# A transformer tower on one core: weight halves, output jobs and base jobs placed anew ahead of and inside the first attention turn

## The reference, cut to what matters

```python
h = s4d_kernel(log_dt, x, B, inv_A_real, A_imag, 1024)     # 64 x 128 x 1024, one row per channel and column of x
a = layernorm(h)                                            # 64 blocks of 128 tokens, 1024 wide
q, k, v = a @ wq.T, a @ wk.T, a @ wv.T                      # 32 query heads, 8 key/value heads, 32 wide
q, k = rope(q), rope(k)
h = h + softmax(causal(q @ k.T / sqrt(32))) @ v @ wo.T      # 128 tokens: every causal key is allowed
y = layernorm(h)
alpha = softmax(log(prior) + y @ router_W.T + router_b)     # 4 active experts
h = h + y @ W_base.T + b_base + sum_e alpha_e * (y @ lora_A_e.T @ lora_B_e.T) * 2
```

## Time and profile before

| | us |
|---|---|
| median of 3 runs | 2940.04 |
| lowest, highest | 2939.99, 2941.34 |
| the profiled execution | 2938.84 |
| its span, first to last instruction | 2937.2 |
| PE busy | 2827.0 (96%) |
| DVE busy | 2436.1 (83%) |
| ACT busy | 1917.3 (65%) |
| POOL busy | 1974.4 (67%) |

### The profile page before, as it was taken

One profiled execution on the slowest core, in us unless ns is written; L12 is line 12 of the kernel. 1 busy time (PEld: TensorE's weight loads), 2 busy tenths in 40 slices (PEclk: granted clock), 3 DMA queues, 4 the chain that ended last, 5 costly groups with the idle time before them and its releaser, 6 DMA issues.

```text
span 2937.2 us, 62768 instructions
## 1 busy us (share of the span) xinstructions
PE 2827.0 (96%) x17444; PEld 1403.3 (48%) x17444; DVE 2436.1 (83%) x8643; ACT 1917.3 (65%) x5982; POOL 1974.4 (67%) x1735
## 2 busy tenths in 40 slices
PE   6788899999999999999999999999999999999987
PEld 5665444444444444444444444444444444444433
DVE  8987788888888888888888888888888888888873
ACT  7987666666666666666666666666666666666662
POOL 4543676777677776777777776677766777677763
PEclk9999899999999999999999999999999999999999
DMA  7884676666666666666666666666666666666652
GB/s 227 241 220 136 136 155 146 149 147 146 151 144 149 147 147 148 148 149 147 148 150 142 148 146 154 148 144 148 145 154 147 146 148 144 151 146 147 144 130 65
DMA packets 1220852, 442.66 MB, mean 151 GB/s; under 512 B 1167120, under 2 KB 1175568, under 8 KB 1220640
## 3 DMA queue, kind: packets, MB, share of 16 engines
q1 hardware_dynamic: 1220640, 440.69, 66.2%
HBM read 88.22 MB, written 67.11 MB: 53 GB/s over the span
## 4 chain that ended last, share of the span: by engine, by line
PE 59%; DVE 15%; issue 9%; POOL 7%; ACT 7%; DMA 1%; SPq 0%; DVEq 0%; ACTq 0%; POOLq 0%
PE bank_b L1763 29%; PE bank_a L1763 16%; PE bank_c L1763 6%; ACT probs L1337 4%; DVE heads L1543 3%; DVE probs L1489 3%; POOL p_hl L1250 3%; PE score L1728 3%; POOL probs L1246 3%; PE pv L1752 2%; PE kps L565 1%; POOL rope_a L1256 1%; DVE share L1498 1%; POOL xy_hl L1265 1%; DMA tok_h<-kout 1%
## 5 line engine op out<-in xcount | busy, mean ns | idle before, releaser
L1337 ACT ACTIVATE probs<-probs,negmax 128x128 f32<-128x128 f32 x2048 | 789.8, 387 | 253.3 <-DVE negmax L1489 253.2
L1250 POOL TENSOR_TENSOR p_hl<-probs,p_hl 128x512 f16<-128x512 f32 x512 | 615.5, 1202 | 340.3 <-ACT p_hl L1346 338.1
L1246 POOL TENSOR_TENSOR probs<-probs,rsum 128x512 f32<-128x512 f32 x512 | 556.6, 1087 | 221.2 <-DVE rsum L1500 220.1
L1763 PE MATMUL bank_a<-qkv_hi,xt 128*128 128x512 f16 x2048 | 652.1, 380 | 1.0 <-DMA xt<-xy_hl 1.0
L1489 DVE CUSTOM_DVE_ANT_0 probs<-score,table,scal 128x128 f32<-128x128 f32 x2048 | 597.5, 347 | 45.4 <-issue 44.8
L1763 PE MATMUL bank_b<-b_hi,yt 128*128 128x512 f16 x2016 | 630.9, 379 | 0.0
L1346 ACT ACTIVATE p_hl<-probs 128x512 f16<-128x512 f32 x512 | 319.8, 625 | 417.6 <-POOL probs L1246 417.6
L1543 DVE TENSOR_TENSOR heads<-rope_a,heads 128x512 f16<-128x512 f32 x320 | 397.8, 1259 | 29.9 <-ACT heads L1367 29.9
L1763 PE MATMUL bank_b<-o_hi,at_hi 128*128 128x512 f16 x1024 | 389.7, 381 | 1.5 <-ACT at_hi L1352 1.5
L1763 PE MATMUL bank_b<-o_lo,at_hi 128*128 128x512 f16 x1024 | 389.9, 381 | 0.0
L1763 PE MATMUL bank_b<-o_hi,at_lo 128*128 128x512 f16 x1024 | 389.7, 381 | 0.0
(11 more groups left out here) (209 smaller groups left out, 4598.8 us busy)
## 6 DMA issues: line engine op xcount, KB each, us to landing
hin<-tok_h SPq DMA_DIRECT2D x64, 512.0 KB, 3.3
r<-tok_h SPq DMA_DIRECT2D x64, 512.0 KB, 3.9
out_dram<-r SPq DMA_DIRECT2D x63, 512.0 KB, 3.0
tok_h<-kout SPq DMA_DIRECT2D x60, 512.0 KB, 6.1
probs_t<-p_hl SPq DMA_TRANSPOSE x512, 3.1
xc<-in_x_dram SPq DMA_DIRECT2D x32, 128.0 KB, 4.5
raw_a<-in_L_attn_wq_dram SPq DMA_DIRECT2D x4, 1024.0 KB, 8.9
raw_b<-in_L_attn_wo_dram SPq DMA_DIRECT2D x8, 512.0 KB, 5.5
```

Of the source, the lines that this page charges most:

```text
L1246: TT(x, x, rsum[:, u % 4].unsqueeze(2).to_broadcast([P, GR, T]), ALU.mult).then_inc(s_norm, 1)
L1250: TT(p_hl[:, u % 2, 1], probs[:, u % 4], p_hl[:, u % 2, 0], ALU.subtract).then_inc(s_plo, 1)
L1337: ins = A(probs[:, u % 4, g], probs[:, u % 4, g], ACT.Exp, bias=negmax[:, u % 4, g:g + 1], scale=-1.0, accum_out=sums[:, u % 4, g:g + 1])
L1763: ins = MM(bank, x(c), w[:, c, cols], start=(c == 0 and i == 0), stop=(c == KC - 1 and i == 2))
```

## The change

Four things are moved; no instruction is added or removed in number, apart from waits.

- DVE makes the low halves of jobs 10 to 13 in `begin`, so ahead of the norm statistics of block 0.
- `pe_close` holds jobs 30 to 35 (`LATE` = 36). The output jobs 36 to 39 move into turn 0, which then has 20 jobs, in the units as 1, 1, 4, 3, 3, 3, 3, 2. PE runs them at the end of a unit, behind its product (`jobs_of`). Jobs 36 to 41 use the banks 2 and 3 in turn, where 38 and 39 had the banks of the scores.
- The statistics of the base weight move from DVE's turn -1 to unit 0 of turn 0, `spread` behind job 37 at the end of unit 1, and `powers(2)` to unit 1.
- In turns 0 and 1 (`spare`) the second query product has 1 step ahead of `scores(3)`, 3 behind it and 4 behind `scores(4)`.

```diff
+    LATE = MID + 6
+    per_slot = (1, 1, 4, 3, 3, 3, 3, 2)
+    SLOTS = [(LATE + sum(per_slot[:k]), LATE + sum(per_slot[:k + 1])) for k in range(8)]
...
         if j < MID:
             return (0, 1, 5, 7)[j % 4]
-        return (j - MID) % 4 if j < J_B else 2 + (j - J_B) % 3
+        if j < LATE:
+            return (j - MID) % 4
+        return 2 + (j - LATE) % 2 if j < J_B else 2 + (j - J_B) % 3
...
             if b == -1 and k == "last":
-                Prep.high(act, MID + 4, J_B)
+                Prep.high(act, MID + 4, LATE)
             if b == 0 and k != "norm" and k != "last":
-                Prep.high(act, J_B + 2 * k, J_B + 2 * k + 2)
+                Prep.high(act, *SLOTS[k])
...
-                low(4, 10)
+                low(4, 14)
 
             def after():
-                low(10, J_O)
+                low(14, J_O)
...
                 if b == -1 and k == "last":
                     low(MID, MID + 4)
+                if b == -1 and k == "end":
+                    low(MID + 4, LATE)
+                if b == 0 and k == 0:
                     dve.wait_ge(s_sums, NO)
                     V.tensor_reduce(mx[:, 2:3], part_max[:, 0:NO], AX_X, ALU.max).then_inc(s_mx, 1)
                     columns(2)
-                if b == -1 and k == "end":
-                    low(MID + 4, J_B)
-                if b == 0 and k == 0:
+                if b == 0 and k == 1:
                     powers(2)
...
                 if b == 0 and isinstance(k, int):
-                    low(J_B + 2 * k, J_B + 2 * k + 2)
+                    low(*SLOTS[k])
...
-            Prep.turn(pe, MID, J_B)
+            Prep.turn(pe, MID, LATE)
...
-                    if u == 0 and not some(b):
-                        prep.spread(pe, 2)
-                    if not some(b):
-                        prep.turn(pe, prep.jb + 2 * u, prep.jb + 2 * u + 2)
+
+                def jobs_of(u):
+
+                    if attention and not some(b):
+                        prep.turn(pe, *prep.slots[u])
+                        if u == 1:
+                            prep.spread(pe, 2)
...
                 if qkv:
                     q(0, 0, 6)
+                jobs_of(1)
...
                 if rest:
                     attend(1)
-                if qkv:
-                    q(1, 0, 5)
+                spare = attention and not finish
+                if qkv:
+                    q(1, 0, 1 if spare else 5)
+                jobs_of(2)
 
                 if attention:
                     scores(3)
                 if qkv:
-                    q(1, 5, 8)
+                    q(1, 1 if spare else 5, 4 if spare else 8)
...
+                jobs_of(3)
 
                 if attention:
                     scores(4)
+                if qkv and spare:
+                    q(1, 4, 8)
...
+                jobs_of(4)
```

More of the change, by code:

```diff
@@ L662, in prepare_weights @@
         done_a, done_c, done_score, done_pv = last_a + 1, last_c + 1, (last[0] + 1, last[1] + 1), last[4] + 1
-        jb, jend, mid = J_B, J_END, MID
+        jb, jend, mid, slots = J_B, J_END, MID, SLOTS
         @staticmethod
@@ L1830, in turn @@
                     kv(0, 7)
+                jobs_of(0)
                 if attention:
@@ L1884, in turn @@
                                         id16[:, :]).then_inc(s_zt, 1)
+                jobs_of(5)
                 if attention:
@@ L1896, in turn @@
                     wo(1, 0, 1)
+                jobs_of(6)
                 if attention:
@@ L1901, in turn @@
                     wo(1, 1, 8)
+                jobs_of(7)
             turns(pe, turn)
```

## The result

| | us |
|---|---|
| before, median of 19 runs (lowest, highest) | 2940.81 (2939.69, 2945.58) |
| changed, median of 19 runs (lowest, highest) | 2947.61 (2945.43, 2950.06) |
| ratio, 95% interval | 1.0023 (1.0017 to 1.0030) |
| changed, profiled execution and its span | 2948.72, 2947.0 |

The changed kernel is 6.8 us slower. That is inside the range of 2938.0 to 2948.0, 3.5 above the forecast of 2944.1, and just over the bound of 0.2%, so on the side that had 0.17. Of these 3.5, 0.8 is the kernel before itself: 2940.81 over 19 runs, and 2940.04 over the three runs that the forecast began from. As a change, +6.8 stands against a forecast of +4.1.

What follows compares the result with a forecast made beforehand. PE holds 59% of the chain, but turn 0's waits form a ring over DVE and ACT, so turn 1's start counts. Opening +0.4, turn 1's start +3.8, query product -0.1: +4.1 on 2940.04 gives 2944.1 us; range 2938.0 to 2948.0.

Steps and rivals of the forecast that it cites:

- the opening: Four low halves ahead of block 0's norm statistics: jobs 18 to 21 at the low clock, +0.4 us, bounds 0 and 1.0.
- The frame: Start of turn 1: a delay or gain there goes through to the end nearly whole, under 4 us idle PE behind it.
- The start of the change: Statistics and four output jobs leave turn -1, so `maxima(0)` of turn 0 starts 2.9 us earlier.
- Rival A: Turn 0: DVE's waits hide the added jobs' lows, so the start's gain stays; -2.6 us, 2937.4; chance 0.13.
- C: Opening, 223.7 to 238 us: PE is the last link, up to 3.9 us gained; -6.5 with A's gain, 2933.5; chance 0.03.
- Units 1 and 2: Turn 0: `maxima(1)` 2.0 us early and `maxima(2)` 1.2 early, the opening's 0.4 not counted.
- Unit 2 to 3: Turn 0: jobs 40 and 41 wait for banks 2 and 3; `maxima` goes from -1.2 to +0.6 us.
- rival B: Units 2 and 3: clock falls behind the new pause, `q(1)` matmuls take 9.1 for 4.5; +6.5 us, 2946.5; chance 0.15.
- The sign that I named for B: A clock under 0.9 in the window of units 3 and 4 would show the main case wrong.
- Units 4 to 7: Turn 0: added jobs make `maxima` +1.9, +2.5, +3.1, +3.8 us late; turn 1 begins +3.8 late.
- the ring: Turn 0: `maxima`, `exps`, highs on ACT, lows on DVE, next `maxima`; one low more costs 0.65 us in units 5 to 7.
- The product's term: Second query product moved: nothing in turn 0; in turn 1 `scores(3)` goes earlier, -0.1 us, bounds 0 to -0.3.

Runs made afterwards that it cites:

- the extra low half: The kernel before, with one more low half made on DVE in each of units 3 to 6 of turn 0; 2945.03 us, ratio 1.0008.
- the filled pause: The changed kernel with 15 matmuls of 512 columns, read by nobody, in PE's pause ahead of `scores(0)`; 2947.1 us, ratio 1.0015.

## Why the prediction was off where it was

**The number is in the range, 0.4 us from its end, and this is partly luck.** The path was right. The terms for the opening and for unit 2 were 0.6 and 1.0 too small, that for unit 6 0.5 too large; the clock behind `scores(0)` had no term, and neither had the 1.2 us and more that are lost behind the first `zt`.

**The frame held.** What is late at turn 1 goes through: +4.68 at its `maxima(2)`, +5.54 at the first `zt`. The start of the change was sized rightly: from +1.02 to -1.95 at `maxima(0)` is -2.97, where the sum had -2.9, and it is spent by unit 3. Rival A had this gain stay; it is not seen in any kernel with the four jobs moved. C falls with the opening.

**The opening: +0.4 was +1.0, my upper bound.** I took the middle of 0 and 1.0. In fact the statistics came 0.6 late, not 0.2: counted like the rows of before, the high halves 10 to 13 end at 220.89 and not at 220.7, and their low halves, 0.68 each, at 221.92. The ten low halves behind the pause took 0.71 each, and the clock was low up to job 18 and into it:

```profile
227.70:231.80 4.10, 0.40 (x2) 0.41 (x3) 1.21 (x2) 4.10 (x6) 1.74 (x1) 0.50 0.19 58
```

**Units 1 and 2 were 0.3 late by themselves**: -1.7 and -0.9 without the opening, against -2.0 and -1.2.

**Unit 2 to 3: the step was +1.8, it was +2.8.** This is the largest wrong term. The wait of 2 us for `o_lo` ahead of job 40 came, with 2.67. What I left out of the sum is the clock behind it: jobs 40 and 41 took 1.94 us, where two base jobs in the kernel before took

```profile
282.66 1.04 PE L908 MATMUL wt<-const,raw_a 128*128 128x128 f32 x8
```

and `scores(3)` took 0.63 in place of 0.39. The second execution of the changed kernel confirms the price. There the clock fell later behind the same wait:

```profile
287.49 1.35 PE L914 MATMUL wt<-const,raw_a 128*128 128x128 f32 x8 [2.67 <-DVE o_lo L815]
```

The two jobs are 0.59 us shorter, and so is the step: +2.20 in place of +2.79. I had the fall as rival B, but with its price on `q(1)`; there, in the first execution, the clock was soon back:

```profile
288.12 0.63 PE L1772 MATMUL bank_c<-qkv_lo,xt 128*128 128x512 f16 x1
288.54 0.76 PE L1772 MATMUL bank_c<-qkv_hi,xt 128*128 128x512 f16 x2
289.14 0.38 PE L1772 MATMUL bank_c<-qkv_lo,xt 128*128 128x512 f16 x1
```

In the second it stayed low over seven matmuls of `q(1)`, up to 292.0, and the step to `maxima(4)` was +1.22 in both. So B's place was right (0.66 from 285 to 290 us), its mechanism was not: the low clock cost where PE itself was the last link, in the two jobs ahead of `scores(3)`, and nothing in PE's slack. The sign that I named for B, a clock under 0.9 over units 3 and 4, is 0.91 in the first execution (287.3 to 296.7) and 0.82 in the second (288.6 to 298.1), with 1.00 in the kernel before (282.4 to 288.8). The Trainium skill, "TensorE: Matmul & The Clock Gate", Part 1: The HAM clock gate, has the clock follow how busy PE has been recently. The trace agrees as far as the fall behind the pause goes, with this 0.66; how long it lasts is what the rows had to say.

**Units 4 to 7: 1.3, 0.6, 0.6, 0.7, 0.0 were 1.2, 0.6, 0.1, 0.7, 0.0.** The sizes are right but for unit 6. The reason I gave, that each wait of DVE lies on the ring, is right in whole for two units of four only: behind unit 5 POOL takes a part of the price, and behind unit 4 the extra low half costs 0.05, and the high half carries the price.

**Missed altogether: the pause ahead of `scores(0)`.** I had `scores(0)` at 262.4 and looked at what DVE had to do before it, not at how long PE had nothing. PE had done its six jobs; the 3.22 us are the last two highs on ACT behind the base sums. In some executions the clock falls there (five of seven profiles), and the product piece of 21 matmuls, 4.53 at full clock, makes `maxima(1)` 1.7 to 2.7 us later. The two profiles of the changed kernel are at +5.54 and +7.99 at the first `zt`, at +6.72 and +10.56 at the last, and the second one's time, 2951.59, is above all 19 runs of the result. The 6.8 us of the medians fit if most of the 19 were like the first profile; how many were is not known. That this clock makes up the rest of the loss is an argument, not shown: the filled pause points that way, inside its interval.

**Turn 1 gave back 0.8** by its `maxima(2)`, within my bound of 1 us. This is not the query product, which stands behind that place. The product's term, -0.1, was right: from `maxima(2)` to `maxima(3)` of turn 1 the lateness falls by 0.14 in the changed kernel, by 0.13 in its second execution, and by 0.00 with the product where it was. The 0.8 are the clock. PE needs 5.70 us from turn 1's `scores(0)` to `scores(1)` in the changed kernel and 6.69 before: the clock comes back after the third matmul of the product, and before only after the eighth or so. The second execution of the changed kernel needs 6.58 there, and gives nothing back.

## What to carry to other kernels

A job moved out of a full stage into a stage full of waits costs its whole price if the waits are links of a ring. Which engine's copy of it carries the price can change from unit to unit, so add it engine by engine. Look at the last slot before the next stage first: with it empty, and all ten output jobs ahead of turn 0, the first `zt` came 2.2 us earlier than in the kernel before. And when work is taken from TensorE ahead of a chain, price the pause that it leaves, by how the clock stood behind pauses of that length in the trace, and in more than one execution: the same pause had both outcomes here.

## What the runs showed of the hardware

The clock can fall or hold behind the same pause of the same kernel: the 3.22 us ahead of `scores(0)` were followed by 1.00 in two profiles and by 0.50 in three, and pauses of 1.33 and 1.48 us there, with a second one of 1.11 or 0.82 for the turned activations behind `scores(0)`, by 0.52 and 0.59. Where the wait was 0.80 or 0.81 us, it held in all five.

An instruction of DVE with two inputs from SBUF can wait for one of POOL's. In the kernel before, in unit 5, the `share`, 0.16 us in the unit ahead of it, takes 0.70 and ends at 297.82; POOL's `xy_hl` ends at 297.80. The next, `lp`, ends with POOL's `rope_a`. DVE, then POOL:

```profile
297.12 0.70 DVE L1498 TENSOR_TENSOR share<-sums,small 128x4 f32<-128x4 f32 x1 [0.45 <-ACT probs L1337]
...
297.95 1.09 DVE L871 TENSOR_TENSOR lp<-prs,prior_row 128x4 f32<-128x4 f32 x1
```

```profile
295.68 2.12 POOL L1265 TENSOR_TENSOR xy_hl<-xyn,xy_hl 128x1024 f16<-128x1024 f32 x1
297.76 1.26 POOL L1256 TENSOR_TENSOR rope_a<-rope_a,rope_b 128x512 f32<-128x512 f32 x1
```

In the changed kernel `share` comes 0.1 us before POOL's end and takes 0.16; with one low half more it takes 0.35, and ends at 299.56, POOL's `xy_hl` at 299.55. These 0.54 and 0.35 us are what made the third step there 0.1 and 0.3 in place of 0.66. The Trainium skill, "SBUF — State Buffer", SBUF: two separate sides, says that the two engines share a pair of ports by a lock that is held for a whole instruction; the rows agree, with ends that lie 0.01 and 0.02 us apart.
